# Joining a feed-forward stage with the first routing pass in a four-layer kernel on one core

## The reference, cut to what matters

```python
    y = _groupnorm_complex(y, gn_scale, gn_bias)
    y = y * silu_g
    y = (y @ Wo.astype(jnp.complex64)).real
    x = _layernorm(x + y, ln1_scale, ln1_bias)
    h = jax.nn.gelu(x @ W1 + b1)
    out = x + (h @ W2 + b2)
    return _layernorm(out, ln2_scale, ln2_bias)
...
    gate_logits = jnp.einsum('te,ex->tx', x, gate_kernel)
    weights, selected = jax.lax.top_k(gate_logits, TOP_K)
    weights = jax.nn.softmax(weights.astype(jnp.float32), axis=-1)
    flat_experts = selected.reshape(-1)
    sort_idx = jnp.argsort(flat_experts)
...
x = x + _L0_attn_ref(_layernorm(x, axis=-1), ...)
x = x + _L0_ffn_ref(_layernorm(x, axis=-1), ...)
```

## Time and profile before

| | us |
|---|---|
| median of 3 runs | 3214.25 (3213.52 to 3217.51) |
| the profiled execution | 3196.49 |
| its span (first to last instruction) | 3194.7 |

### The profile page before, as it was taken

One profiled execution on the slowest core, in us unless ns is written; L12 is line 12 of the kernel. 1 busy time (PEld: TensorE's weight loads), 2 busy tenths in 40 slices (PEclk: granted clock), 3 DMA queues, 4 the chain that ended last, 5 costly groups with the idle time before them and its releaser, 6 DMA issues. The chain is left out here.

```text
span 3194.7 us, 36195 instructions
## 1 busy us (share of the span) xinstructions
PE 2642.7 (83%) x12202; PEld 1809.3 (57%) x12202; DVE 1914.6 (60%) x3369; ACT 1097.8 (34%) x1765; POOL 1375.3 (43%) x862
## 2 busy tenths in 40 slices
PE   6773499854999999997588897888878677997998
PEld 3331366644999999997233343333433334666997
DVE  6999678463212122222989999998999995331211
ACT  6775122100111111111555645546455431221111
POOL 0000234345333333332168778687786850112332
PEclk9886699955999999998699998999989888998999
DMA  3000100012899999986300010000100001116996
GB/s 114 0 0 0 45 13 20 13 41 98 318 324 325 324 325 327 319 308 223 106 33 34 27 34 33 33 34 27 36 31 33 34 27 34 40 40 239 349 347 238
DMA packets 95181, 395.13 MB, mean 124 GB/s; under 512 B 21366, under 2 KB 48518, under 8 KB 72544
## 3 DMA queue, kind: packets, MB, share of 16 engines
q1 hardware_dynamic: 73472, 351.46, 31.4%
q0 software_dynamic: 21600, 42.37, 3.6%
HBM read 364.94 MB, written 39.29 MB: 127 GB/s over the span
## 5 line engine op out<-in xcount | busy, mean ns | idle before, releaser
L1331 POOL TENSOR_TENSOR ss_h<-ss_h,ss_cs 128x2048 f32<-128x2048 f32 x127 | 574.4, 4525 | 75.1 <-DVE ss_h L1721 67.1
L1418 PE MATMUL ss_y<-ss_h,all_ident 128*128 128x512 f32 x1016 | 520.3, 661 | 49.3 <-POOL ss_h L1331 49.3
L1176 DVE TENSOR_TENSOR experts_in<-experts_sil,experts_pU 128x512 f32<-128x512 f32 x176 | 121.3, 689 | 635.4 <-PE experts_pU L1120 635.4
L1721 DVE TENSOR_TENSOR_SCAN ss_h<-ss_da,ss_c_h,ss_dbu 128x512 f32<-128x512 f32 x384 | 470.8, 1268 | 7.1 <-ACT ss_da L1575 0.3
L1418 PEld LDWEIGHTS ss_y<-ss_h,all_ident 128*128 128x128 f32 x1016 | 213.3, 214 | 323.0 <-issue 260.9
L1575 ACT ACTIVATE ss_da<-ss_dt,ss_decay 128x512 f32<-128x512 f32 x512 | 326.7, 711 | 103.7 <-DVE ss_h L1721 65.2
L1714 DVE TENSOR_TENSOR ss_dbu<-ss_dtx,ss_bB 128x1024 f32<-128x1024 f32 x256 | 314.5, 1229 | 62.2 <-PE ss_bB L1408 36.3
L1120 PE MATMUL experts_pG<-experts_xt,experts_wa 128*128 128x128 f32 x2816 | 346.5, 277 | 0.9 <-DMA experts_wa<-in_w_all 0.9
L1120 PE MATMUL experts_pU<-experts_xt,experts_wa 128*128 128x128 f32 x2816 | 344.1, 275 | 0.0
L1129 PE MATMUL experts_pY<-experts_wa,experts_in 128*128 128x256 f32 x1408 | 332.7, 379 | 0.0
L1120 PEld LDWEIGHTS experts_pG<-experts_xt,experts_wa 128*128 128x128 f32 x2816 | 331.6, 193 | 1.7 <-ACT experts_xt L1146 1.1
(11 more groups left out here) (327 smaller groups left out, 3681.6 us busy)
## 6 DMA issues: line engine op xcount, KB each, us to landing
experts_wa<-in_w_all SPq DMA_DIRECT2D x176, 1536.0 KB, 9.1
ss_cs<-ss_c_rows SPq DMA_DIRECT2D x64, 512.0 KB, 3.6
moe_rows<-route_xn SPq DMA_DIRECT2D x16, 512.0 KB, 3.7
ss_h<-moe_ys SPq DMA_DIRECT2D x5, 1024.0 KB, 7.7
all_x<-in_x SPq DMA_DIRECT2D x8, 512.0 KB, 9.1
gf_xb<-in_x SPq DMA_DIRECT2D x8, 512.0 KB, 3.8
moe_rows<-all_x SPq DMA_DIRECT2D x8, 512.0 KB, 3.6
experts_xr<-moe_rows,moe_token POOLq DMA_INDIRECT x176, 8.0
```

The costliest lines, as they stand in the source:

```text
L1176: nc.vector.tensor_tensor(IN[t.two][:].rearrange("p f t -> p (f t)"), SIL[t.two][:], pU[t.two][:], ALU.mult)\
L1331: pool.tensor_tensor(h[:], h[:], CS[q % 2][:, n % GROUP].unsqueeze(1).to_broadcast([P, CI, BT]), ALU.mult)\
L1418: mm = pe.matmul(y[:, c], ident[:], H[(b * N + n) % RING][:, c], start=(n == 0), stop=(n == N - 1))
L1721: ins = V.tensor_tensor_scan(H[(b * N + n) % RING][:, c], DA[(b * N + n) % AHEAD][:, c], DBU[:, c % 2], first, ALU.mult, ALU.add)
```

## The change

`gate_ffn` and the first `route` become one function, `gate_ffn_route`, in one block with one barrier and one clearing of semaphores (49, where `gate_ffn` had 24 and this `route` 25). Its loop is unrolled in Python over NB + 3 = 11 steps. In step i block i is in its Wo part, block i-1 in the W1 and W2 halves, block i-2 in its routing rows and logits, block i-3 in choice, ranks and slots. The second `route` stays as it was.

```diff
+                wait(pe, "wo_loaded", 16)
+                for i in STEPS:
+                    if inside(i):
+                        wo(i)
+                    if i == 0:
+                        fold()
...
+                    if inside(i - 1):
+                        ffn_up(i - 1)
+                    if inside(i - 3):
+                        ranks(i - 3)
+                    if inside(i - 1):
+                        ffn_down(i - 1)
+                    if inside(i - 2):
+                        route_turn(i - 2)
+                    if inside(i):
+                        turn(i)
+                    if inside(i - 2):
+                        logits(i - 2)
```

VectorE's order in a step is choose(i-3), first(i), the statistics of the routing rows, place(i-3), z(i+1), second(i-1):

```diff
+                for i in STEPS:
+                    if inside(i - 3):
+                        choose(i - 3)
+                    if inside(i):
+                        first(i)
...
+                    if inside(i - 2):
+                        route_rows(i - 2)
+                    if inside(i - 3):
+                        place(i - 3)
+                    if inside(i + 1):
+                        z(i + 1)
+                    if inside(i - 1):
+                        second(i - 1)
```

`route_rows(b)` waits for out(b), takes the statistics of that block alone and ends with one more small operation, the shift. The rows are normalised on ScalarE, and its order is 8 Gelus, four rows, two routing copies, two copies of the first norm's transposes:

```diff
+                def normalise_route(b):
+                    wait(act, "rows_ready", b + 1)
+                    wait(act, "rxt_raw", b - 1)
...
+                    for j in range(TPB):
+                        A_(RXN[b % 2][:, j], X[:, b * TPB + j], ACT.Identity, scale=route_rstd[:, j:j + 1], bias=route_shift[:, j:j + 1])\
+                            .then_inc(s["rxn_done"], 1)
...
+                for i in STEPS:
+                    if inside(i - 1):
+                        gelu(i - 1)
+                    if inside(i - 2):
+                        normalise_route(i - 2)
+                        copy_route(i - 2)
+                    if inside(i):
+                        copy_xt(i)
```

The first norm's scale and bias go into the weights. TensorE transposes X1N, the row before scale and bias; W1 is scaled once, row by row, on ScalarE; TensorE multiplies the bias with W1 once (`fold`), and VectorE adds it to b1. POOL adds b2 to the bias row once and then has two operations per block where it had three, in place in X:

```diff
+                    wait(pe, "x1n_done", i * TPB + TPB)
...
+                ch.link(pool.tensor_tensor(rows["ln1b"][:], rows["ln1b"][:], rows["b2"][:], ALU.add))
...
+                def x1(i):
+
+                    wait(pool, "x1n_done", i * TPB + TPB)
+                    pool.tensor_tensor(blk(X, i), X1N[:], row("ln1s"), ALU.mult).then_inc(s["halved"], 1)
+                    wait(pool, "halved", i + 1)
+                    pool.tensor_tensor(blk(X, i), blk(X, i), row("ln1b"), ALU.add).then_inc(s["residual_done"], 1)
...
+                    for f in range(FC):
+                        for k in range(KD):
+                            mm = pe.matmul(pH[0][:, f:f + 1], W1[:, k, f * P:(f + 1) * P], ln1b[:, k:k + 1], start=(k == 0), stop=(k == KD - 1))
...
+                for k in range(KD):
+                    A_(W1[:, k], W1[:, k], ACT.Copy, scale=ln1s[:, k:k + 1]).then_inc(s["scaled"], 1)
```

More of the change, by code:

```diff
@@ L1776, in build @@
             gate_loop(nc, g["x"], g["w_proj"], X, YS, SG, SUMS, ident, (r0, r1))
-            gate_ffn(nc, g, X, YS, SG, SUMS, ident)
-        route(nc, "route0", X, g["router0"], r0, ident)
+            gate_ffn_route(nc, g, X, YS, SG, SUMS, g["router0"], r0, ident)
         expert_tiles(nc, "experts0", r0, g["w_all0"], ident)
```

555 lines of the change are left out of this document (353 added, 202 removed).

## The result

The joined kernel took 3139.74 us (median of 4 runs, 3137.00 to 3142.22) beside 3215.69 us for the kernel before: ratio 0.9764, 95% interval 0.9752 to 0.9775, a gain of 76 us. The profiled execution took 3140.11 us, its span is 3138.4 us.

The account below looks back on a forecast made before the run. TensorE bounds the feed-forward stage; routing then follows serially at half clock. 122.7 - 38.9 - 28.8 - 2.0 = 53 us gain; 3196.5 profiled becomes 3143, plus 17.8 gives a median of 3161 us, range 3149 to 3183.

Parts of the forecast that it names:

- The clock term: TensorE's clock falls behind the routing stretch at 5/7 of six places, 1.7 us each: +7.3 us, bounds 0 and 10.
- the clock holds: Rival: no clock loss at the routing stretch of the joined loop; gain 60 us, 3154 us, chance 0.17.
- The frame: 122.7 us from last W2 product to last slots, less what remains; median set 17.8 us above the profiled execution.
- step: TensorE's steady step in the joined loop grows from 33.0 to 37.05 us, 38.3 with the clock.
- ranks: Between W1 and W2 on TensorE, 1.6 us at full clock, hiding the Gelu gap: +0.65 us, six times.
- logits wait: TensorE waits 0.7 us for ScalarE's copies of the routing transposes before the logits in each step.
- D8 late, without the clock: Delay of the last W2 product's end from routing transposes, logits and ranks, less the first norm; 28.8 us with the clock.
- the first norm: First block's transposes no longer wait for POOL's scale and shift: -1.4 us at stage start, nothing in the steady step.
- D8 to last slots: From the end of the last W2 product, remaining routing to the last slots: 38.9 us, 37.4 unblocked, at half clock.
- last slots to first weights, more than before: The last barrier clears 49 semaphores instead of 25: +2.0 us, bounds 0 and 2.1; finishing the lists stays 21 us.
- choice, row statistics, place on VectorE: VectorE per step: choice 3.5 to 9.0 us beside POOL, statistics 5.1 plus up to 3.1, place 2.1.
- just inside: VectorE keeps up with TensorE's step: blocked sum 37.0 us, slack 3.4 us at the routing rows.

Follow-up runs that it names:

- e6: Joined kernel with the first norm's transposes ahead of the routing transposes, so nothing covers ScalarE's copies: 3140.55 us beside 3196.50 for the kernel before.
- e5: Joined kernel with the routing rows normalised by VectorE instead of ScalarE: 3135.51 us beside 3196.50 for the kernel before.
- e7: Joined kernel with the ranks behind W2 and VectorE's gated rows of the next block ahead of the place: 3163.03 us beside 3198.22 for the kernel before.
- e4: Joined kernel without the folding (W1 unscaled, three POOL operations per block, transposes wait for POOL): 3142.42 us beside 3196.50 for the kernel before.
- e12: The kernel before, unchanged, run once more on another chip: 3220.53 us beside 3217.49.
- e2: The joined kernel, unchanged, run again beside the kernel before: 3134.36 us beside 3197.36, ratio 0.9802.
- e3: Joined kernel with the ranks behind W2 instead of between W1 and W2: 3176.84 us beside 3196.50 for the kernel before.
- e13: Joined kernel without the folding and with the routing rows normalised by VectorE, second run: 3148.37 us beside 3216.31 for the kernel before.

## Why the prediction was wrong

Forecast 3161 us, range 3149 to 3183; measured 3139.7. The direction was right, the size too small by 21 us. Two steps failed, of about 7 and 12 us; the other terms make up the rest.

**The clock term.** "0.28 x 6 us = 1.7 us lost each ... 5/7 x 6 x 1.7 = +7.3" measured 0: the clock is 1.00 in all the windows up to the last step, and in e6 with a longer wait too. The rival "the clock holds" is what came, and 60 us of gain was its number; 62 to 63 was measured in the short comparisons (its 3154 us missed all the same, by the frame). The term had been carried over by its share from a stage in which other things differ as well. That the idle time was only 0.30 us instead of 0.7 isn't the whole reason, as 1.17 us cost no clock either; what decides stays open, since 1.24 us (e5) and 1.90 us (e7) did cost some, and 1.91 us (e4) did once and once not. The Trainium skill, TensorE: Matmul & The Clock Gate, section Part 4: PE-mode transpose, which says that transposes don't count as busy in the same way, would have made it 10; the trace doesn't bear that out here: 1.7 us of transposes, 0.3 or 1.17 us idle and the logits cost the clock nothing between W2 and Wo.

**The frame.** "One like it would take 3143; the median ... is 3214.25, 17.8 above, and the forecast for the median is 3161": this carried the 17.8 us over to the new kernel. They were no property of all the kernel: the long execution that was traced (e12) has 18.8 us of stalls in the very pass that the change removes, and the joined kernel has 4.0, so about 5 us were to be carried over, not 17.8. Worked out from the profiled execution, with the sum's own 60 us without the clock term, the forecast would have been some 3137 us and 4 more in a long comparison. That the profiled execution lay 17 us or more below every timed run was the sign, and the prediction took it for an offset.

The other terms, against the undisturbed execution of the joined kernel (e2: stage start 338.73, D8 653.97, last slots 692.45, first weights 715.41):

| term | predicted us | measured us |
|---|---|---|
| step | 37.05 without the clock (37 to 38.8 as the sign) | 36.76 |
| ranks (behind W1, W2 without a gap) | 1.6 | 1.57 |
| logits wait | 0.7 | 0.30 idle |
| D8 late, without the clock | 21.5 | 20.3 |
| of it the first norm | -1.4 | -0.9 |
| D8 to last slots | 38.9 | 38.5 |
| last slots to first weights, more than before | +2.0 | +1.6 |
| choice, row statistics, place on VectorE | 9.0, 8.2, 2.1 | 8.4, 7.6, 2.1 |
| VectorE's rows ahead of the routing transposes | 3.4 slack | 3.5 to 3.9 |

122.7 - 20.3 - 38.5 - 1.6 = 62.3 us, which is what the stage gained. Of the 1.6 us, 1.5 lie between the last row of the lists and the first weights, where barrier and clearing are (5.0 us before, 6.5 after); that the 24 more semaphores make them was not tested.

**VectorE** was called "just inside" by its slack of 3.4 us at the routing rows. That number came out and was not the one that counts. The hand-over that bites first is the second norm's additions, which free the logits' bank: there VectorE has 0.5 to 0.9 us to spare, and e3, e4, e5 and e7 all show TensorE released by gf_r at the logits. The prediction named what queues behind the routing rows and left this one out. The folding, which "only frees VectorE" in the steady step and was given nothing there, is worth about 7 us with the start of the stage, because without it VectorE sets the step (1.5 us of the 7 are the start, and part of the rest is the clock behind the waits). The blocked operations, priced from the earlier trace rows, came within 0.6 us: one such operation of VectorE held by each of POOL.

## What to carry to other kernels

When work of two stages is joined, price each engine's order and not its busy time: the moved piece belongs where the engine that consumes it is busy with something else, since one in-order wait (here 8.07 us at the place) passes through everything queued behind it to the engine that sets the time. Small edits that take an operation off a second engine are worth little while it has slack (e5, 2 us) and nearly all of it once it has none (e13), so count the slack at every buffer that is handed back, also at those that merely free a bank. If the profiled execution lies far from the median, find in which stage the difference lies before carrying it over as a constant.

## What was not expected of the hardware

- Waits of 1.17 us between transposes and logits, in four steps looked at (e6), left the granted clock at 1.00. Behind waits of 1.24 us (e5) and 1.90 us (e7) Wo took 5.36 us, and behind 4.32 us (e3) 4.79, instead of 3.67; the clock of the step was 0.96, 0.96 and 0.92. Of two waits of 1.91 us in e4 one had Wo at 3.67 us behind it and one at 5.13, so the length of the wait alone doesn't say it.
- The four one-hot operations took 4.8 us together beside POOL's arithmetic and 0.74 us without it (POOL still or at its list transfers); MAX8 and FIND_INDEX8, which read the logits' bank, took 0.62 and 0.22 us in either case.
- The same kernel before had executions of 3197 us in three comparisons and of 3216 us in three, the difference being, where it was traced, waits for which the profile names no engine of the program, in one stage. The cause is open; that they cost the joined kernel 4 us and the separate pass 19 us is shown by one trace of before and two of after.
